# Who writes the second copy of the attended values: ScalarE from PSUM, or GpSimd inside the SBUF

## The reference

```
h   = layernorm(x)                                    # (8, 512, 256)
q   = h @ Wq;  k = ctx @ Wk;  v = ctx @ Wv            # 8 heads of 64, 1024 keys
a   = softmax(q k^T / 8) v                            # "attended values", per head
x   = x + tanh(g0) * (a @ Wo + bo)
h   = layernorm(x);  router picks 2 of 8 experts per token, capacity 1.25
x   = x + tanh(g1) * experts(h)                       # silu-gated, 1024 wide
```

## Time and profile before

| quantity | value |
|---|---|
| median of 3 runs | 1755.44 us (1754.02 to 1757.16) |
| the profiled execution | 1759.72 us |
| its span, first to last instruction | 1758.0 us |
| mean granted TensorE clock | 0.994 of full speed |
| PE / PEld busy | 1681.4 / 1532.0 us |
| DVE / ACT / POOL busy | 1267.5 / 1053.8 / 684.9 us |
| attention pipeline | up to about 1090 us, 132.0 us per middle batch |

### The profile page before, as it was taken

One profiled execution on the slowest core, in us unless ns is written; L12 is line 12 of the kernel. 1 busy time (PEld: TensorE's weight loads), 2 busy tenths in 40 slices (PEclk: granted clock), 3 DMA queues, 4 the chain that ended last, 5 costly groups with the idle time before them and its releaser, 6 DMA issues.

```text
span 1758.0 us, 35339 instructions
## 1 busy us (share of the span) xinstructions
PE 1681.4 (96%) x13198; PEld 1532.0 (87%) x13198; DVE 1267.5 (72%) x2666; ACT 1053.8 (60%) x2233; POOL 684.9 (39%) x623
## 2 busy tenths in 40 slices
PE   6999999999999999999999998999999999999997
PEld 5778888888888888888888877999999999999997
DVE  6888888888888888888888887575555455555443
ACT  5767767767767767766766765445445444544443
POOL 3352444444444444444444426214343323233323
PEclk9999999999999999999999999999999999999999
DMA  4300210210210210210210223232332413221211
GB/s 123 122 25 1 103 56 25 102 58 25 101 58 25 99 60 25 97 63 25 93 54 26 93 102 107 75 94 44 96 103 36 103 31 102 69 64 31 30 31 24
DMA packets 59834, 114.39 MB, mean 65 GB/s; under 512 B 6920, under 2 KB 47760, under 8 KB 59056
## 3 DMA queue, kind: packets, MB, share of 16 engines
q1 hardware_dynamic: 43600, 93.37, 15.0%
q0 software_dynamic: 16096, 19.19, 6.2%
HBM read 88.67 MB, written 57.95 MB: 83 GB/s over the span
## 4 chain that ended last, share of the span: by engine, by line
PE 75%; DVE 10%; issue 5%; POOL 3%; ACT 3%; DMA 2%; another core or an unknown queue 0%; POOLq 0%; DVEq 0%; SPq 0%
PE ring L1174 11%; PE turned L1068 11%; PE ffn L1031 10%; PE ffn L1032 10%; PE ffn L1033 10%; PE scores L1056 9%; DVE neg_max L1786 5%; PE ring L1031 4%; PE ring L1033 3%; PE ring L1032 3%; DVE pt_l L1563 2%; PE ring L1140 1%; PE ring L1142 1%; POOL probs L864 1%; POOL rows L817 1%
## 5 line engine op out<-in xcount | busy, mean ns | idle before, releaser
L864 POOL TENSOR_SCALAR probs<-probs,row_rec 128x1024 f32<-128x1024 f32 x254 | 283.3, 1129 | 472.5 <-DVE row_rec L1889 461.2
L1355 ACT ACTIVATE pt_h<-turned 128x512 fp32r<-128x512 f32 x512 | 279.8, 603 | 208.9 <-PE turned L1068 208.9
L1563 DVE TENSOR_TENSOR pt_l<-turned,pt_h 128x512 fp32r<-128x512 f32 x512 | 331.3, 681 | 7.2 <-ACT pt_h L1355 6.9
L1786 DVE TENSOR_REDUCE neg_max<-scores 128x1 f32<-128x1024 f32 x256 | 301.6, 1218 | 36.3 <-PE scores L1056 36.2
L1068 PE MATMUL turned<-ident,probs 128*128 128x128 f32 x2048 | 281.9, 279 | 25.9 <-DVE pt_l L1563 18.6
L1068 PEld LDWEIGHTS turned<-ident,probs 128*128 128x128 f32 x2048 | 224.1, 141 | 94.0 <-issue 65.6
L1411 ACT ACTIVATE probs<-scores,neg_max 128x1024 f32<-128x1024 f32 x256 | 285.4, 1118 | 9.9 <-DVE neg_max L1786 9.9
L1174 PE MATMUL ring<-pt_h,v_hl 128*128 128x256 f32 x1024 | 261.3, 293 | 0.2
L2113 DVE TENSOR_TENSOR act_f<-ffn,silu 128x256 f32<-128x256 f32 x288 | 122.0, 424 | 179.7 <-ACT silu L1510 167.6
L1174 PE MATMUL ring<-pt_l,v_hl 128*128 128x256 f32 x1024 | 250.8, 283 | 0.0
L1510 ACT ACTIVATE silu<-ffn 128x256 f32<-128x256 f32 x288 | 110.5, 384 | 219.5 <-PE ffn L1033 205.4
(11 more groups left out here) (243 smaller groups left out, 4070.5 us busy)
## 6 DMA issues: line engine op xcount, KB each, us to landing
lists<-pads SPq DMA_DIRECT2D x8, 4160.0 KB
w_raw<-w_t SPq DMA_DIRECT2D x14, 1024.0 KB, 10.6
e_rows<-lists SPq DMA_DIRECT2D x37, 260.0 KB
ctx_raw<-ctx_t SPq DMA_DIRECT2D x15, 512.0 KB, 3.6
wg_raw<-wg_t SPq DMA_DIRECT2D x7, 1024.0 KB
x_in<-x SPq DMA_DIRECT2D x8, 512.0 KB, 4.0
x_sum<-x SPq DMA_DIRECT2D x8, 512.0 KB, 3.9
out<-x_sum SPq DMA_DIRECT2D x8, 512.0 KB, 2.9
```

The lines of the kernel that those rows point to most:

```text
L864: nc.gpsimd.tensor_scalar(probs[:, k, :], probs[:, k, :], row_rec[:, k:k + 1], 1.0, ALU.mult, ALU.mult).then_inc(scaled, 1)
L1355: return nc.scalar.activation(dst, src, ACT.Copy)
L1563: return nc.vector.tensor_tensor(dst, src, hi_part.bitcast(F32), ALU.subtract)
L1786: nc.vector.tensor_reduce(neg_max[:, k:k + 1], scores[:, n % 2, :].rearrange("p (a c) -> p a c", a=2), AX.XY, ALU.max, negate=True).then_i ...
```

## The change

ScalarE drains an "o" with one copy, into `ot_h`. A new function on GpSimd's queue, `copy_high`, waits for that copy (semaphore `hi_o`) and copies rows 0 to 63 of `ot_h` into rows 0 to 63 of `ot_x`. It stands in GpSimd's `step` behind the scaling and ahead of all else in that step. PE's "w" jobs get a further wait, on the count of such copies (`ot_copied`). VectorE's instructions are the same.

```
+            def copy_high(body, u):
+                for (kind, i, _), _ in body.results(u):
+                    if kind == "o":
+                        h, m = i // 4 * 2 + i % 2, i // 2 % 2
+                        toks = slice(m * 2 * P, (m + 1) * 2 * P)
+                        wait_hi(pool, "o", body.b - 1 if u <= 5 else body.b, i)
+                        alone(pool)
+                        nc.gpsimd.tensor_copy(ot_x[0:DH, h % 4, toks], ot_h[0:DH, h % 4, toks])\
+                            .then_inc(ot_copied, 1)
...
                                                     ALU.mult, ALU.mult).then_inc(scaled, 1)
+                    copy_high(body, u)
                     if body is FIRST and u == 3:
...
                     o = ("o", H * i + H // 2 + 1 + j // 2 * 2, 0)
                     reads = [body.before.where[o] - RING if i == 1 and j < 2 else body.where[o]]
+                    pe.wait_ge(ot_copied, at(b - 1 if i == 1 else b, 2 * H, o[1] + 1))
...
                     toks = slice(m * 2 * P, (m + 1) * 2 * P)
-                    hi(ot_x[0:DH, h % 4, toks], bank[0:DH, 0:2 * P])
                     last = hi(ot_h[:, h % 4, toks], bank[:, 0:2 * P])
```

More of the change, by code:

```diff
@@ L421, in build @@
         early_here = sem("early_here")
+        ot_copied = sem("ot_copied")
         early_scaled = sem("early_scaled")
```

## The result

| | before | after |
|---|---|---|
| median, us | 1754.86 (1754.02 to 1757.16) | 1781.31 (1779.25 to 1782.18) |
| ratio, 95% interval | | 1.0149 (1.0137 to 1.0160) |
| profiled execution, its span | 1759.72, 1758.0 | 1780.62, 1778.9 |
| mean granted clock of PE | 0.994 | 0.989 |

The forecast was 1761.8, in 1754.5 to 1768.5. The sign was right. The size was not: +26 us came, +6.4 were forecast. Between the two profiled executions the difference is 20.9 us. What follows is read from the two traces, so it accounts for the 20.9.

The account below looks back on a forecast made before the run. PE, busy 96% of the span, was taken as the bound, so only its few waits count. Terms -2.2 + 2.4 + 2.1 + 2.4 + 1.7 = +6.4 us on a 1755.44 us median gave 1761.8 us, range 1754.5 to 1768.5.

Parts of the forecast that it names:

- What is removed: Part on ScalarE's 128 dropped copies: 48 us busy time, ScalarE 0.28 us ahead per "o", 36 us in all.
- in most places this dies at once: ScalarE's 0.28 us per "o" gains nothing in most places; the chain uses its `ot_x` only eight times.
- nearly all of the 58 us lie in idle time: GpSimd idles 61% of the span, so its 128 new copies mostly cost nothing, except at four places.
- Relief, -2.2 forecast: First and last batch: eight chain places times 0.28 us gained, bounds 0 and 2.7 us.
- The copy's price, 0.45: One 64x256 copy on GpSimd, by a straight line between other row sizes; between 0.34 and 0.56 us.
- Step 22, +2.4: Six middle batches: copy delays L801, which holds VectorE's L1646 ahead of PE's "x" job, 0.4 us each; bounds 0 to 3.4.
- Step 0, +2.4: Six middle batches: step 30's copy delays scatters, their landing and step 0's scaling, 0.4 us each; bounds 1.5 to 3.4.
- Step 11, +2.1: Batches 1 to 7: copy and VectorE's L1612 collide, delaying `normalise` and PE by 0.3 us each; bounds 0 to 3.9.
- END, +1.7: Last two copies behind ten `low_first` stall PE 5.1 us before the third "w"; net 1.7 us, bounds 0 and 3.4.
- the half-clock stretch at 1102: END: new stall may bring half clock forward, adding 1.5 to 1.7 us; sparing the later stretch gives 1.7 back.
- the experts, put at nothing: Expert part behind END: nothing is changed there, so no term.
- the rivals: Copy that blocks nobody, 1757.8 us, chance 0.24; relief that reaches PE, 1751.4 us, 0.14; dear copy, 1774 us, 0.07.

Follow-up runs that it names:

- copies alone: Changed kernel with ScalarE's second copy kept, so GpSimd overwrites rows 0 to 63 of `ot_x` with the same values: 1785.13 us, ratio 1.0147.
- nudged kernel: Kernel before plus one 128x1 VectorE `memset` ahead of the router's two-input operation in the middle batches: 1771.23 us, ratio 1.0069.
- order settled by a wait: Changed kernel; at step 24 GpSimd waits for VectorE's thirteenth router operation ahead of the second `split_ctx`: 1766.95 us, ratio 1.0047.
- relief alone: Kernel before with ScalarE's single copy from the ninth "o" on, no GpSimd copies, high rows of `ot_x` left stale: 1772.77 us, ratio 1.0082.
- copies moved: Kernel with step 24's wait and END's copies moved up, plus copies of steps 11, 22, 23 and 30 placed later: 1757.37 us, ratio 1.0003.
- END's copies moved up: Changed kernel with step 24's wait, END's two copies behind the fourth and fifth `low_first` instead of the tenth: 1760.62 us, ratio 1.0021.

## Why the size was wrong

**The step that failed** is in "What is removed": of ScalarE's 0.28 us per "o", "in most places this dies at once". It was tested on which engine PE waits for. VectorE was named there, and so I left ScalarE. The freed time did die as work, but it lives as a shift between two engines: `row_rec` came 0.06 us sooner against VectorE's own work. The same sentence lies behind "nearly all of the 58 us lie in idle time" of GpSimd. The rule that would have found it was in the prediction's hands, for it was used at steps 11 and 22: I asked it only of GpSimd's instructions next to a new copy. The `split_ctx` of step 24 is one step behind the place of the earlier trace rows, and its neighbour on VectorE is the same line of code. It cost 6 x (0.44 + 1.52) = 11.8 us and 4.3 us of half clock. The copies alone did the same, so both halves of the change, the relief put at a gain and the copies put at idle time, had this price missing.

The Trainium skill ("SBUF — State Buffer", Who interferes with whom) has the rule and also its sharp end: the order of issue decides who waits, not the shape of the operation. The traces of before and after agree: the same operation took 0.18 us where it was first, and 1.05 where it was second, behind an instruction of 1.06. In four meetings of the nudged kernel it was held though its recorded start came first, by 0.01 to 0.02 us; there the traces can neither confirm the rule nor refute it.

**Relief, -2.2 forecast.** About -0.9 in the first batch, from 20 us to its last steps; 0.5 us more were won before the first "o" had been drained, by chance. The middle batches, put at nothing, gave nothing that lasts. The last batch can't be told from its half-clock stretch. Too high, since the chain's other engines fill in behind.

**The copy's price, 0.45.** 0.39 us, a straight line between rows of other sizes was good enough.

**Step 22, +2.4.** The place is as told, the size a third of it, 0.8 us. On GpSimd, then VectorE and PE, of the changed kernel:

```profile
648.03 0.40 POOL L843 CAST ot_x<-ot_h 64x256 fp32r<-64x256 f32 x1
...
649.52 2.40 POOL L802 TENSOR_TENSOR ctx_l<-ctx_raw,ctx_h 128x1024 fp32r<-128x1024 f32 x1
...
651.63 0.33 DVE L1659 TENSOR_TENSOR gate<-gate 128x32 f32<-128x32 f32 x1
...
654.17 0.63 PE L1160 MATMUL ring<-ident,x_in 128*128 128x128 f32 x4 [1.45 <-DVE ot_x L1576]
```

L802 ends at 651.92, L1659 at 651.96 after 0.33 us instead of 0.18: held 0.15, not 0.4. Two things were taken too large. Against PE's lateness of 7.6 us the copy pushed L802 by 0.3 us, not 0.45; and a held operation ends 0.04 us behind GpSimd's (here, and twice at step 24), where the prediction had it held first and then run. So it ends 0.10 us late, and PE's "x" job is 0.12 later. PE's lateness in batch 4, counted from just ahead of step 12 (times of before), tells this from step 11's part:

| kernel | 599.3 | 602.9 | 605.4 | 634.9 | "x" job, 646.5 |
|---|---|---|---|---|---|
| after | +0.20 | 0.00 | +0.20 | +0.19 | +0.31 |
| order settled by a wait | +0.21 | +0.02 | +0.21 | +0.21 | +0.35 |
| copies alone | +0.24 | +0.04 | +0.24 | +0.24 | +0.37 |
| relief alone | 0.00 | -0.19 | +0.01 | +0.01 | -0.02 |
| copies moved | -0.02 | -0.19 | -0.01 | -0.01 | -0.03 |

The other five middle batches have the same to within 0.1 us. Of the 0.34 us per batch between steps 12 and 22, 0.2 are step 11's and the remaining 0.1 to 0.15 step 22's.

**Step 0, +2.4.** With the order settled it cost 0.44 to 0.49 in each batch, 2.8 us: there the mechanism and the size are right. In the changed kernel itself the delay is there and is given back. Its timeline:

```profile
687.18 0.39 POOL L843 CAST ot_x<-ot_h 64x256 fp32r<-64x256 f32 x1
...
694.49 2.23 POOL L876 TENSOR_SCALAR probs<-probs,row_rec 128x1024 f32<-128x1024 f32 x2 [1.47 <-DMA lists<-rows,list_row]
...
695.66 0.86 PEld L1081 LDWEIGHTS turned<-ident,probs 128*128 128x128 f32 x8 [0.77 <-POOL probs L876]
```

PE waits 0.77 in place of 0.36 us and is 0.44 later, and four microseconds on 0.32 of it are won back. In the row above all six batches come to 0.5 us, so in the kernel that was forecast the term was five times too large. It isn't the wait that decides: with it and END's copies moved up, the delay was given back for the most part in five batches of six. What decides is open.

**Step 11, +2.1.** Read as forecast, and worth 0.2 us in each middle batch, 1.3 us in six:

```profile
738.84 0.40 POOL L843 CAST ot_x<-ot_h 64x256 fp32r<-64x256 f32 x1 [4.13 <-ACT ot_h L1369]
738.88 0.36 DVE L1625 SCALAR_TENSOR_TENSOR norm<-mean_var,norm 128x4 f32<-128x4 f32 x1
...
739.45 2.17 POOL L818 TENSOR_SCALAR rows<-x_sum,norm 128x256 f32<-128x256 f32 x4 [0.22 <-DVE norm L1625]
...
742.77 1.09 PE L1081 MATMUL turned<-ident,probs 128*128 128x128 f32 x8 [0.66 <-POOL probs L876]
```

VectorE's operation is held by the copy and ends with it (0.36 us, has 0.15); `normalise` follows, and PE waits 0.66 instead of 0.46. The 0.2 us stay: the table above has them at 599.3, 605.4 and 634.9 in each kernel with this copy in its place, and in none without it. At 602.9 all five kernels of the table are 0.2 us nearer to before, with the copy and without it, so that dip gives nothing back. The mechanism was right; 0.3 was taken for 0.2.

**END, +1.7.** The stall was forecast at 5.1 us, net +1.7; it is 4.8, net +2.1. Of GpSimd, VectorE and PE:

```profile
1107.64 3.65 DVE L1576 TENSOR_TENSOR act_l<-act_f,act_h 128x256 fp32r<-128x256 f32 x1 [0.48 <-ACT act_h L1369]
...
1110.27 0.74 POOL L843 CAST ot_x<-ot_h 64x256 fp32r<-64x256 f32 x2
...
1111.06 0.58 PE L1154 MATMUL ring<-wo_h,ot_h 128*128 128x256 f32 x1 [4.79 <-POOL ot_x L843]
...
1113.24 0.48 DVE L1770 SCALAR_TENSOR_TENSOR x_sum<-ring,tanh_g,x_sum 128x256 f32<-128x256 f32 x1 [1.96 <-PE ring L1156]
```

The matmuls behind it ran at half clock for 5.4 us, which cost 2.5 (1.5 to 1.7 were forecast), the two waits of before near 1100 became none, and the half-clock stretch at 1102 was spared, as the prediction set out.

So the sum of what was looked at is right, +6.8 for +6.4 with the order settled, and partly by luck: steps 11 and 22 cost 2.1 for 4.5, while the relief gave 0.9 less than forecast and the experts, put at nothing, cost 1.3. What failed is the list of places. The range rested on the bounds of known terms and had no room for one that was missing; of the rivals none was this one.

## What to carry to other kernels

Before relieving or delaying an engine, list each pair of a GpSimd instruction and a two-SBUF-input instruction of VectorE whose starts lie within a few tenths in the trace of before, over the whole loop and not only where the edit stands; such a pair is decided by hundredths, and the loser pays the other's full length. If one order is cheap and the other dear, fix it with a wait ahead of the long instruction. Then put added work behind whatever hurries on its queue: moving four of the sixteen copies of a batch gave 3 us back.

## What the runs showed of the hardware

A VectorE operation of 128x32 with two SBUF inputs can take 0.18 or 1.05 us, and 0.06 us of delay decide it. So these two engines meet at more than the semaphores that the first section names. Such an operation can be held over several GpSimd instructions in a row: sent in the last 0.3 us of one subtraction, `act_l` took 3.65 us beside two more and two copies, until 0.28 us after the last copy ended. The recorded start of a held operation need not be the time from which it works, for in the nudged kernel it lies 0.01 to 0.02 us ahead of the instruction that held it. And of six stalls of PE of 1.6 us, alike in the trace, three were followed by 3.4 us at 1.2 GHz (one of six with the relief alone, three of six with the copies alone, two of four in the nudged kernel); what tells them apart is not to be seen in these rows.
